# Short products into one z bank, and two score tiles side by side for one exponential

## The reference, cut to what matters

```
x: (2, 2048, 256); 16 heads of 64; causal attention
q, k, v = x W_Q, x W_K, x W_V                 per head
scores  = q k^T / 8, masked above the diagonal
probs   = softmax(scores)                      over the keys
z       = probs v
x1 = layernorm(x + concat(z) W_out + b_out)
x2 = layernorm(x1 + 0.5 * (silu(ln(x1) W1 + b1) W2 + b2))   (1024 hidden, dequantised weights)
```

## Time and profile before

| | |
|---|---|
| median of 3 runs | 2101.74 us (2098.75 to 2102.37) |
| profiled execution, its own time | 2106.1 us |
| span of the profile | 2104.3 us |
| TensorE busy | 1852.2 us, 88% |
| ScalarE busy | 1522.4 us, 72% |
| VectorE busy | 1442.9 us, 69% |
| GpSimd busy | 1399.3 us, 66% |
| mean granted TensorE clock | 0.968 of 2.4 GHz |

### The profile page before, as it was taken

The page is one execution under the profiler, slowest core; times in us unless marked ns, Lnnn a source line. Parts: engine busy times, 40 slices in busy tenths (PEclk is TensorE's granted clock), DMA queues, the critical chain, the costliest instruction groups (busy, mean ns, idle before and its releaser), DMA issues. The chain is left out here.

```text
span 2104.3 us, 46244 instructions
## 1 busy us (share of the span) xinstructions
PE 1852.2 (88%) x18249; PEld 1278.6 (61%) x18249; DVE 1442.9 (69%) x2688; ACT 1522.4 (72%) x3151; POOL 1399.3 (66%) x866
## 2 busy tenths in 40 slices
PE   3788988998989898989898989898999986988997
PEld 2454655565656565656565656565656555878886
DVE  3886867685868686767676767767676838565553
ACT  1577786878787878788787878787878782564454
POOL 2365766777768686868686868776868786443242
PEclk9899999999999999999999999999999997998998
DMA  3001010001010101010101010101010205111220
GB/s 105 16 4 52 28 41 2 17 26 37 6 41 2 41 2 41 3 40 4 39 4 39 7 36 9 34 9 34 10 33 12 91 3 204 61 61 61 70 71 21
DMA packets 48616, 74.56 MB, mean 35 GB/s; under 512 B 5904, under 2 KB 32784, under 8 KB 48144
## 3 DMA queue, kind: packets, MB, share of 16 engines
q1 hardware_dynamic: 48400, 71.59, 10.7%
HBM read 33.82 MB, written 20.97 MB: 26 GB/s over the span
## 5 line engine op out<-in xcount | busy, mean ns | idle before, releaser
L452 POOL TENSOR_TENSOR p_lo<-p_full,p_hi 128x1024 f16<-128x1024 f32 (+1 forms) x640 | 1167.2, 1839 | 427.1 <-ACT p_full L511 425.4
L510 ACT ACTIVATE p_hi<-psum 128x512 f16<-128x512 f32 (+3 forms) x1280 | 710.9, 555 | 268.5 <-PE psum L774 145.4
L550 DVE TENSOR_REDUCE row_max<-psum 128x1 f32<-128x512 f32 (+3 forms) x1280 | 725.7, 603 | 107.8 <-PE psum L736 58.1
L511 ACT ACTIVATE p_full<-psum 128x512 f32<-128x512 f32 (+3 forms) x1280 | 719.4, 562 | 0.0
L793 PE MATMUL psum<-v,p_hi 128*128 128x129 f16 x4352 | 521.6, 221 | 56.5 <-DVE z_sum L590 51.3
L795 PE MATMUL psum<-v,p_lo 128*128 128x65 f16 x4352 | 493.8, 193 | 0.0
L793 PEld LDWEIGHTS psum<-v,p_hi 128*128 128x128 f16 x4352 | 401.8, 98 | 143.4 <-issue 72.8
L736 PE MATMUL psum<-ka,qa 128*128 128x512 f16 (+3 forms) x1280 | 441.1, 353 | 41.7 <-DVE kb L580 16.0
L768 PE MATMUL psum<-qa,ka 128*128 128x512 f16 (+3 forms) x1280 | 446.0, 350 | 15.2 <-ACT p_full L511 10.4
L772 PE MATMUL psum<-qb,kb 128*128 128x512 f16 (+3 forms) x1280 | 446.5, 349 | 0.0
L795 PEld LDWEIGHTS psum<-v,p_lo 128*128 128x128 f16 x4352 | 391.2, 98 | 63.3 <-issue 1.3
(11 more groups left out here) (125 smaller groups left out, 2913.5 us busy)
## 6 DMA issues: line engine op xcount, KB each, us to landing
zT_dram<-z_T SPq DMA_DIRECT2D x16, 1024.0 KB, 4.2
shared_z<-zT_dram SPq DMA_DIRECT2D x28, 512.0 KB, 6.4
qb<-qa SPq DMA_DIRECT2D x128, 64.0 KB, 1.9
ka<-ka SPq DMA_DIRECT2D x128, 64.0 KB, 1.9
shared_z<-xT_dram SPq DMA_DIRECT2D x8, 512.0 KB, 6.2
xs<-x_dram SPq DMA_DIRECT2D x8, 512.0 KB, 5.6
out_dram<-shared_w SPq DMA_DIRECT2D x8, 512.0 KB, 3.3
w_raw_rest<-wqkv_dram SPq DMA_DIRECT2D x1, 2304.0 KB, 14.0
```

What stands on the lines that cost most here:

```text
L452: nc.gpsimd.tensor_tensor(p_lo[:, at % NP, cols], p_full[:, at % NP, cols], p_hi[:, at % NP, cols], ALU.subtract).then_inc(probs_split, 1)
L510: nc.scalar.activation(p_hi[:, at % NP, to], lane_bank(a)[:, P * f:QB], ACT.Exp, scale=1.0 / SCORE)
L511: nc.scalar.activation(p_full[:, at % NP, to], lane_bank(a)[:, P * f:QB], ACT.Exp, scale=1.0 / SCORE).then_inc(lane_read, 1)
L550: nc.vector.reduce_max(row_max[:, n % MAXES, t, c:c + 1], bank_of(r)[:, 0:chunk_width(n, t, c)], AX.X).then_inc(ring_read, 1)
```

## The change

- Products: three matmuls instead of two. p_hi against 65 columns (one, v hi), p_hi against the 64 columns of v's lo part, added into the same 64 columns of z, and p_lo against 65. So z has 65 columns a query tile, and a block's four tiles fit one bank (`Z_BANKS = 1`).
- outputs: VectorE takes the reciprocal, waits for it, and multiplies z in PSUM by it straight into z_pair. GpSimd's normalise, z_sum and the `z_read` semaphore go; the bank is free with `z_done`.
- Lanes: two of two banks each (2 x 2 lanes + 3 ring + 1 z = 8). The two tiles of a step stand side by side in one lane, which is counted once for a step and once for an out. `lane_ready` comes with the second tile. TensorE waits for the lane only ahead of the first tile.
- probs: once a step, at the place of the second tile in the order, over both tiles (1024 columns, or 640 on the diagonal).

```diff
@@ -38,6 +38,7 @@
...
 VS = VW + 1
+VZ = C + 1
 START = 1
...
@@ -101,8 +102,9 @@
...
 MAXES = 4
+Z_BANKS = 1
 RINGS = 3
-LANES = 3
+LANES = 2
...
@@ -256,7 +258,7 @@
...
-    counted = [x for x in ORDER if x[0] in kinds]
+    counted = [x for x in ORDER if x[0] in kinds and (x[0] != "scores" or x[3] == 0)]
     return {x: r for r, x in enumerate(counted)}
@@ -322,7 +323,7 @@
...
         psum = ctx.enter_context(nc.psum_tensor("psum", [P, 8, QB], F32))
-        LANE, RING, Z = 0, LANES, LANES + RINGS
+        LANE, RING, Z = 0, 2 * LANES, 2 * LANES + RINGS
...
@@ -356,7 +357,13 @@
...
         def lane_bank(a):
-            return psum[:, LANE + a % LANES, :]
+            return LANE + 2 * (a % LANES)
+
+        def lane_view(a):
+            return psum[:, lane_bank(a):lane_bank(a) + 2, :].rearrange("p k t -> p (k t)")
+
+        def z_bank(at):
+            return psum[:, Z + at % Z_BANKS, 0:TPB * VZ].rearrange("p (t w) -> p t w", t=TPB)
...
@@ -448,24 +455,13 @@
...
                 cols = slot_cols(*SLOTS[i])
-                pool.wait_ge(lane_read, lane_place("scores", m, i, 1) + 1)
+                pool.wait_ge(lane_read, lane_place("scores", m, i) + 1)
                 nc.gpsimd.tensor_tensor(p_lo[:, at % NP, cols], p_full[:, at % NP, cols], p_hi[:, at % NP, cols],
                                         ALU.subtract).then_inc(probs_split, 1)
-
-            def normalise(m, n):
-
-                h, q = block_of(n)
-                pool.wait_ge(z_read, m * NBLK + n + 1)
-                if m:
-                    pool.wait_ge(lane_ready, lane_place("out", m - 1, q) + 1)
-                nc.gpsimd.tensor_tensor(z_pair[:, TPB * q:TPB * q + TPB, h, :], z_sum[:, :, :],
-                                        z_rcp[:, :].unsqueeze(2).to_broadcast([P, TPB, C]), ALU.mult).then_inc(z_done, 1)
...
                     low_probs(m, x[0])
-                if what == "outputs":
-                    normalise(m, *x)
...
@@ -499,16 +495,14 @@
...
-            def probs(m, i, u):
-
-                at, a = m * NSLOT + i, lane_place("scores", m, i, u)
-                _, _, f = slot_tiles(*SLOTS[i])[u]
-                to = slice(tile_col(u, f, f), tile_col(u, f, TPB))
-                if u == 0:
-                    reach(act, slot_used, at - NP + 1)
+            def probs(m, i):
+
+                at, a = m * NSLOT + i, lane_place("scores", m, i)
+                cols = slot_cols(*SLOTS[i])
+                reach(act, slot_used, at - NP + 1)
                 act.wait_ge(lane_ready, a + 1)
-                nc.scalar.activation(p_hi[:, at % NP, to], lane_bank(a)[:, P * f:QB], ACT.Exp, scale=1.0 / SCORE)
-                nc.scalar.activation(p_full[:, at % NP, to], lane_bank(a)[:, P * f:QB], ACT.Exp,
+                nc.scalar.activation(p_hi[:, at % NP, cols], lane_view(a)[:, cols], ACT.Exp, scale=1.0 / SCORE)
+                nc.scalar.activation(p_full[:, at % NP, cols], lane_view(a)[:, cols], ACT.Exp,
                                      scale=1.0 / SCORE).then_inc(lane_read, 1)
...
@@ -526,8 +520,8 @@
...
                     group(m, *x)
-                if what == "scores":
-                    probs(m, *x)
+                if what == "scores" and x[1] == 1:
+                    probs(m, x[0])
                 if what == "out":
...
@@ -582,14 +576,16 @@
...
+                h, q = block_of(n)
+                at = m * NBLK + n
                 dve.wait_ge(slot_used, m * NSLOT + SLOTN[n] + 1)
-
-                reach(dve, z_done, m * NBLK + n)
-                z = psum[:, Z:Z + 2, 0:2 * VW].rearrange("p k (t w) -> p k t w", t=2)
-                nc.vector.reciprocal(z_rcp[:, :].rearrange("p (k t) -> p k t", k=2), z[:, :, :, 0])
-                nc.vector.tensor_reduce(z_sum[:, :, :].rearrange("p (k t) c -> p k t c", k=2),
-                                        z[:, :, :, 1:VW].rearrange("p k t (a c) -> p k t c a", a=2),
-                                        axis=AX.X, op=ALU.add).then_inc(z_read, 1)
+                z = z_bank(at)
+                nc.vector.reciprocal(z_rcp[:, at % 2, :], z[:, :, 0]).then_inc(rcp_ready, 1)
+                if m:
+                    dve.wait_ge(lane_ready, lane_place("out", m - 1, q) + 1)
+                dve.wait_ge(rcp_ready, at + 1)
+                nc.vector.tensor_tensor(z_pair[:, TPB * q:TPB * q + TPB, h, :], z[:, :, 1:VZ],
+                                        z_rcp[:, at % 2, :].unsqueeze(2).to_broadcast([P, TPB, C]), ALU.mult).then_inc(z_done, 1)
...
@@ -759,11 +755,12 @@
...
                 h, q = block_of(n)
-                a = lane_place("scores", m, i, u)
-                reach(pe, lane_read, a - LANES + 1)
+                a = lane_place("scores", m, i)
+                if u == 0:
+                    reach(pe, lane_read, a - LANES + 1)
                 _, k, f = slot_tiles(n, s)[u]
                 cols = slice(QB * q + P * f, QB * q + QB)
-                to = lane_bank(a)[:, P * f:QB]
+                to = lane_view(a)[:, tile_col(u, f, f):tile_col(u, f, TPB)]
                 keys = slice(P * k, P * k + P)
...
@@ -772,7 +769,8 @@
...
                     last = nc.tensor.matmul(to[:, 0:P], ident_b[:, :], mask_k[:, :], start=False, stop=True)
-                last.then_inc(lane_ready, 1)
+                if u == 1:
+                    last.then_inc(lane_ready, 1)
...
@@ -787,15 +785,18 @@
...
-                        reach(pe, z_read, m * NBLK + n)
-                    z = psum[:, Z + t // 2, VW * (t % 2):VW * (t % 2) + VW]
+                        reach(pe, z_done, m * NBLK + n - Z_BANKS + 1)
+                    z = z_bank(m * NBLK + n)[:, t, :]
                     cols = slice(tile_col(u, f, t), tile_col(u, f, t) + P)
-                    nc.tensor.matmul(z, p_hi[:, at % NP, cols], v[:, m % 2, k, h, 0:VW], start=(k == 0 and t % 2 == 0),
+                    last = (n, s, u) == last_slot_tile(n, t)
+                    nc.tensor.matmul(z, p_hi[:, at % NP, cols], v[:, m % 2, k, h, 0:VZ], start=(k == 0 and t == 0),
                                      stop=False, skip_group_check=True)
-                    last = nc.tensor.matmul(z[:, 0:1 + C], p_lo[:, at % NP, cols], v[:, m % 2, k, h, 0:1 + C],
-                                            start=False, stop=(n, s, u) == last_slot_tile(n, t), skip_group_check=True)
+                    nc.tensor.matmul(z[:, 1:VZ], p_hi[:, at % NP, cols], v[:, m % 2, k, h, VZ:VW], start=False,
+                                     stop=False, skip_group_check=True)
+                    done = nc.tensor.matmul(z, p_lo[:, at % NP, cols], v[:, m % 2, k, h, 0:VZ],
+                                            start=False, stop=last, skip_group_check=True)
                 if u == 1:
-                    last.then_inc(slot_used, 1)
+                    done.then_inc(slot_used, 1)
...
...
```

More of the change, by code:

```diff
@@ L273, in lane_place @@
 def lane_place(what, m, i, u=0):
-    return LANE_AT[(what, m, i, u) if what == "scores" else (what, m, i)]
+    return LANE_AT[(what, m, i, 0) if what == "scores" else (what, m, i)]
 def attention(nc, shared, early_in, xT, wqkv, zT_dram, wout):
@@ L308, in attention @@
         neg_max = sb("neg_max", [P, 2, TPB])
-        z_rcp = sb("z_rcp", [P, TPB])
-        z_sum = sb("z_sum", [P, TPB, C])
+        z_rcp = sb("z_rcp", [P, 2, TPB])
         z_pair = sb("z_pair", [P, ST, 2, C])
@@ L341, in attention @@
         slot_used = sem("slot_used")
-        z_read = sem("z_read")
+        rcp_ready = sem("rcp_ready")
         z_done = sem("z_done")
@@ L518, in out_rows @@
                 act.wait_ge(lane_ready, a + 1)
-                nc.scalar.activation(z_T[:, q, :], lane_bank(a), ACT.Copy,
+                nc.scalar.activation(z_T[:, q, :], psum[:, lane_bank(a), :], ACT.Copy,
                                      scale=z_scale[:, m // PAIRS, m % PAIRS:m % PAIRS + 1]).then_inc(lane_read, 1)
@@ L805, in turn_outputs @@
                 for u in range(TPB):
-                    last = nc.tensor.transpose(lane_bank(a)[:, P * u:P * u + P],
+                    last = nc.tensor.transpose(psum[:, lane_bank(a), P * u:P * u + P],
                                                z_pair[:, TPB * q + u, :, :].rearrange("p h c -> p (h c)"), ident[:, :])
```

## The result

The changed kernel takes **2124.22 us** (median of 4 runs, 2121.09 to 2125.57) against 2101.64 us before: ratio 1.0108, 95% interval 1.009 to 1.0125. It is 22.6 us slower. That lies inside the range that was given, but the forecast was 2091 us, a gain.

The account below looks back on a forecast made before the run. TensorE was taken to set the pace, at 88% of the span. Terms of +0.2 - 0.4 - 0.4 + 1.0 - 0.6 - 0.5 = -0.7 us a unit, -11 us in all, gave 2091 us; range 2062 to 2150.

Parts of the forecast that it names:

- covered in the middle: Mid-unit, the joined exponential ends a step some 0.5 us later; claimed harmless because products come three steps of about 2.6 us later.
- the tail: Once-a-unit stretch: VectorE idles 5.18 us for ScalarE's ka copy, z waits 2.09 us; joined exponential forecast net -0.4 us a unit.
- the short products: TensorE's product groups: three short matmuls at 29 ns, 88 ns a group against 87.5 a pair, +0.2 us a unit.
- the short matmuls have a floor: Rival, chance 0.22: successive short load-and-matmul pairs on TensorE need over 29 ns; 2137 us at 33 ns, 2230 at 40.
- z and z_pair: Output path: z freed 0.12 us sooner, five waits a unit, -0.6 us; transposes no longer wait for GpSimd's multiplication, -0.5 us.
- Lanes, out and the joined exponential: Per unit: joined exponential -0.4 us in ScalarE's full stretch, second tile's lane wait gone -0.4, out taking a double lane +1.0.
- the wait behind the out: Scores after an out's transposes wait for the preceding step's joined exponentials: new 0.8 us wait once a unit.
- the scores' other waits for p_full: TensorE's score matmuls waiting for a lane: the second tile's wait goes with double lanes, -0.4 us a unit.
- ScalarE's fixed part: Fixed time per exponential on ScalarE, 0.055 us; two fewer a step save 4.4 us of ScalarE a unit.
- coarse steps: Rival, chance 0.15: late exponentials and the out lane cost 1.8 to 2.5 us a unit, tail earns nothing; 2110 to 2126 us.

## Why the prediction was wrong

The step that failed is the cost of the joined exponential: its later start was put at nothing in the middle of a unit, "covered in the middle", since products come three steps later. The runs show 26 us for it, about 1.6 us a unit, with what it earned in the tail already taken off. A second term, the short products, was mis-sized: +0.2 us, measured +0.8. By the prediction's own terms, a unit at a time (16 units; a ratio step of 0.001 is 2.1 us):

- **Products**, +0.2 us: the floor was there. A group takes 92.5 ns where the pair took 87.5 and 88 was forecast, 272 x 5 = 1.4 us of TensorE's time; the run with it alone lost 13 us, 0.8 a unit, as part is taken back in shorter waits. The rival "the short matmuls have a floor" put its turning point at 30.2 ns a matmul; they take 92.5 / 3 = 30.8. The row that I went by, 29 ns behind one short matmul, was right for one and not for three in a row. The Trainium skill (page "TensorE: Matmul & The Clock Gate", section "Back-to-back issue gap") gives 81 ns for a load and a 128-column matmul in a sustained stream. The trace does not agree: 128-column matmuls with a load each (L720 of the kernel before) start 56 ns apart in the median, and those of 64 and 65 columns 31. The first of these rows was there before the prediction and would have settled its doubt about the page.
- **z and z_pair**, -0.6 and -0.5: right in sum. From 1.0061 to 0.9979 is 17 us, 1.1 a unit. The transposes' wait for z_pair (6.9 us in 1200, 0.6 a unit) went whole, and the z waits fell from 38.7 to 33.8 us, 0.4 a unit. The 0.12 us that each z wait was to be shorter is mis-sized: z is free 0.05 us sooner (0.749 to 0.700 us in the mean). The wait for VectorE's own result was put at 0.03 us, and no row shows such a wait; it is 0.10 to 0.11. That the sum fits is in part luck.
- **Lanes, out and the joined exponential**, -0.4 - 0.4 + 1.0 = +0.2: measured +1.7, 27 us, and it alone turns the sign. The double lanes themselves cost next to nothing: with single exponentials in them the scores wait 2.1 us for p_full in 1200 (5.2 before), the longest 0.2. With the joined exponential there are three parts. First, the wait behind the out was foreseen at 0.8 us once a unit and is 0.67 (8.1 of the 14.0 us for p_full in 1200): right in place and size. Second, the scores' other waits for p_full were to shrink by 0.4 a unit and did not: 5.9 us in 1200 against 5.2. Third and largest, I looked at the waits of the scores and not at the transposes' own: at the unit's start their lane is that of the latest step but one, whose exponentials now start with its second tile, and they wait 0.89 us, 10.6 us in 1200. No term of the sum stands for that. These parts and the z waits earned (33.8 to 26.8 us) come to less than 1.7 us a unit; the rest is time that the view does not count as a wait and is not split up here.
- What hid it is that "covered in the middle" holds for p_lo and for the products, which come three steps later. But the lane is taken again two steps on, and behind an out by the very next step, and for these the end of the exponential counts. The run with one exponential for each tile in the same double lanes shows it: 26 of the 27 us.
- **The tail**: the product's wait went from 2.09 to 1.25 us, more than the net 0.4 forecast. The longest z wait is 2.0 us with single exponentials and 1.3 with joined ones, so most of it is the joining's. The gain was there; the late starts took it back elsewhere.
- **ScalarE's fixed part**, 0.055 us by the rows: ScalarE's busy time fell by 62 us for 1280 exponentials fewer, 0.05 us each. The 0.093 us of the Trainium skill (page "ScalarE: Activation LUTs", section "What ACT_TABLE_LOAD costs"), its 186 ns less the overlap of 93, would have been 119 us by that estimate; the runs do not agree with it.

Rival "coarse steps" had the late start of the exponentials, with 2110 to 2126 us and 0.15, and was wrong in that the tail would earn nothing. It came true together with a small floor, and the two were weighed as if only one could be. That 2124 us lies inside the range of 2062 to 2150 is owed to these two rivals and not to the forecast's own terms, which by its own account reached from 2070 to 2105.

## What to carry to other kernels

Joining two instructions of one engine saves its fixed part (0.05 us here) and costs, at every place where that engine was waiting, the time between the first input and the last; look for who is next behind its result (here the lane, one or two steps away) before counting what is three steps away as cover. Where there are two passes over the same data, try joining the later pass only: here p_full over both tiles and p_hi for each gained 0.4% over no joining in the same lanes. Joining the earlier pass alone was not run. And look for a place in the trace where the thing comes in a row: a row that shows one short matmul at 29 ns is no proof for three in a row.

## What the runs showed of the hardware

- Matmuls of 64 or 65 columns with a weight load of 128 columns each follow each other at 30.3 to 31.2 ns in the mean at 2.4 GHz (granted clock 0.99 to 1.00 from 500 to 1700 us), where 65 columns are 27 ns; one alone between longer ones takes 29. Where the three of a group do not all read the same columns, one gap of three is 34 ns; width, the place in PSUM, the data and the order were tried without removing it, and even starts brought it to 32 in one layout and left it at 34 in another.
- Matmuls of 128 columns with a load each start 56 ns apart (L720 of the kernel before).
- Reads of two PSUM banks by one exponential of 1024 columns run at the rate of one bank: starts 0.92 us apart at 1024 columns in the place shown and 0.903 in the median, where two of 512 took 0.95.
- VectorE's wait for its own reciprocal, from its end to the multiplication's start, is 1022.12 - 1021.83 - 0.18 = 0.11 us (0.104 in the mean of 94 places).
